# GpSimd waits for the attention tiles of the next batch at their places in its own order

## The reference

```python
pos = clip(base + s_idx * freq_avg + phase_avg, 0, Ll - 1); lo = floor(pos); hi = min(lo + 1, Ll - 1)
g_lo = xh[b_ix, lo]
g_hi = xh[b_ix, hi]
g = g_lo + frac[..., None, None] * (g_hi - g_lo)
out_h = einsum('blshd,blhs->blhd', g, w)
```

## Time and profile before

| | |
|---|---|
| three runs | 2343.15, 2349.13, 2356.42 us (median 2349.13) |
| the profiled execution: span, first to last instruction | 2353.6 us |
| PE busy | 1720.4 us (73%) |
| DVE busy | 1254.1 us (53%) |
| POOL busy | 1103.7 us (47%), nearly all of it 1056 indirect DMAs |
| ACT busy | 988.0 us (42%) |
| mean granted clock of PE | 0.854 |

### The profile page before, as it was taken

How to read it: one execution, slowest core, us unless ns; L and a number is a source line. 1 busy time by engine, 2 the same in 40 slices (tenths; PEclk the granted TensorE clock), 3 DMA queues, 4 the chain that set the end, 5 groups by cost and what they waited for, 6 DMA issues and landing times.

```text
span 2353.6 us, 31786 instructions
## 1 busy us (share of the span) xinstructions
PE 1720.4 (73%) x12145; PEld 1141.7 (49%) x12153; DVE 1254.1 (53%) x2158; ACT 988.0 (42%) x2363; POOL 1103.7 (47%) x1069
## 2 busy tenths in 40 slices
PE   5787876767777766666776766667787768879866
PEld 3354534445445534344555434454455346656645
DVE  6565645555556444555565545655565454343345
ACT  3365673234543551243353540335354533343333
POOL 0000016475556345664556255554665367766630
PEclk8799998778989877988898978789888879989876
DMA  3010023132223232232223232232233343223321
GB/s 133 10 24 14 19 48 96 58 102 83 79 75 103 63 74 79 79 96 73 88 79 90 56 95 70 83 90 72 86 89 85 69 148 99 88 81 90 88 47 36
DMA packets 93420, 178.72 MB, mean 76 GB/s; under 512 B 21452, under 2 KB 50264, under 8 KB 93016
## 3 DMA queue, kind: packets, MB, share of 16 engines
q0 software_dynamic: 50688, 138.48, 21.4%
q1 hardware_dynamic: 42584, 38.23, 5.8%
HBM read 151.46 MB, written 9.44 MB: 68 GB/s over the span
## 4 chain that ended last, share of the span: by engine, by line
PE 39%; DVE 19%; another core or an unknown queue 18%; ACT 12%; issue 9%; SPq 1%; POOL 1%; DMA 1%; DVEq 0%; POOLq 0%; ACTq 0%
PE c L1612 5%; DVE pool_c L1235 4%; PE pa L1508 3%; PE pb L1508 3%; PE ta L1542 2%; DVE ssq L1132 2%; PE ta L1516 2%; ACT pool_a L771 2%; ACT pool_a L836 2%; PE sc L1587 2%; DVE pool_a L1155 1%; DVE pool_a L1185 1%; PE tb L1389 1%; PE pb L1560 1%
## 5 line engine op out<-in xcount | busy, mean ns | idle before, releaser
L729 POOL DMA_INDIRECT pool_c<-rows_of_x,idx x1056 | 1100.9, 1043 | 1156.5 <-PE c L1612 380.0
L1612 PE MATMUL c<-ident,pool_c 128*128 128x128 f32 x2112 | 337.1, 303 | 61.6 <-DVE pool_c L1235 32.2
L1612 PEld LDWEIGHTS c<-ident,pool_c 128*128 128x128 f32 x2112 | 278.3, 158 | 143.0 <-issue 97.0
L1235 DVE TENSOR_TENSOR pool_c<-pool_c 128x768 f32<-128x768 f32 x352 | 331.3, 951 | 20.1 <-DMA pool_c<-rows_of_x,idx 19.7
L860 ACT ACTIVATE prob<-sc,nmax 128x128 f32<-128x128 f32 x512 | 179.3, 374 | 0.1
L1516 PE MATMUL ta<-ident,pool_a 128*128 128x128 f32 x512 | 90.9, 333 | 90.8 <-DVE pool_a L1155 80.4
L771 ACT COPY pool_a<-tb 128x512 f32<-128x512 f32 x188 | 112.5, 599 | 103.6 <-remote 58.3
L1155 DVE TENSOR_TENSOR pool_a<-ta,rinv 128x512 f32<-128x512 f32 x64 | 44.3, 692 | 199.9 <-remote 158.3
L1542 PE MATMUL ta<-vmix,pool_a 128*64 128x64 f32 x1024 | 80.9, 239 | 81.0 <-ACT pool_a L771 67.5
L1142 DVE TENSOR_REDUCE nmax<-sc 128x8 f32<-128x1024 f32 x64 | 77.5, 1211 | 103.9 <-remote 96.1
L1508 PE MATMUL pa<-wqkv,pool_a 128*128 128x512 f32 x192 | 118.8, 706 | 12.9 <-DVE pool_a L1185 7.4
(11 more groups left out here) (413 smaller groups left out, 3344.3 us busy)
## 6 DMA issues: line engine op xcount, KB each, us to landing
pool_c<-rows_of_x,idx POOLq DMA_INDIRECT x1056
vmix<-vring SPq DMA_DIRECT2D x128, 128.0 KB
rows_of_x<-x2tok SPq DMA_DIRECT2D x16, 256.0 KB
xtok<-in_x SPq DMA_DIRECT2D x4, 512.0 KB
x_of_all<-x2tok SPq DMA_DIRECT2D x8, 256.0 KB
out<-pool_c SPq DMA_DIRECT2D x8, 256.0 KB, 2.3
wqkv<-in_wqkv SPq DMA_DIRECT2D x1, 1536.0 KB
xtok<-x_of_all SPq DMA_DIRECT2D x3, 512.0 KB
```

The costliest lines, as they stand in the source:

```text
L729: pool.indirect_dma_start(gat[:, n % GB, s, :], None, tables[b % 2], bass.IndirectOffsetOnAxis(ap=idx[:, t, SC * c + s:SC * c + s + 1], ax ...
L1235: V.tensor_tensor(g4, g4, wv, ALU.mult).then_inc(SEM["c_prod"], 1)
L1612: ins = mm(out[:, c:c + P], x, ident[:], start=(i == 0 and k == 0), stop=(i == BCH - 1 and k == len(parts) - 1), is_transpose=True, skip_g ...
```

## The change

POOL's function `first` now waits at the steps "S" and "O": it holds POOL's list at that place until PE has written the tile's scores, or its probabilities times values. Gathers that come later in the list are issued after the wait. No other engine's code is changed.

```diff
@@ -710,7 +710,8 @@
             pool.wait_ge(setup["pool"], 1)
 
             def first(b, what, *a):
-                pass
+                if what in ("S", "O"):
+                    wait_filled(pool, (what, *a), b)
 
             def gather(b, n):
 
```

## The result

On the chip of the first comparison the kernel after takes 2323.71 us (median of 8 runs, 2319.04 to 2339.86) and the kernel before 2352.03 (8 runs, 2339.13 to 2361.38): a ratio of 0.9895, 95% interval 0.9865 to 0.9925. The ratios in this document come from executions in the chip's faster state alone, and lie up to 0.3% from the quotient of the medians (here 0.988). The change makes the kernel about 1% faster. I had predicted no change, with a chance of 0.05 for faster.

A forecast was written before the change was run, and what follows sets the result against it. The prediction took the kernel as bound by the to and fro between PE, DVE and ACT. Its terms 0 + 0 + 0 left the median of 2349.13 unmoved: forecast 2349 us, range 2338 to 2361.

The forecast's parts named there:

- None of the 90 gathers is held by a tile: Gathers of chunks 31 to 87, batches 0 to 2, behind one new wait: tile already signalled when needed; cost 0.
- A met wait costs 0, by chunk 21's 0.30 us: Chunk 21's gather, already with a second wait, starts after the usual 0.30 us pause, so an extra met wait adds 0.00.
- Chunk 44: Gather with a second, long met wait; its pause of 0.69 to 1.80 us was not put down to that wait.
- my bounds: Cost of one met wait on POOL: taken as 0, upper end 1.50 us, no lower end below nothing.
- What hides it: Each of the 90 gathers leads its product by at least 11.64 us; POOL has some 119 us per batch to catch up.
- Rival 1: Chunks 31 to 87, batches 0 to 2: POOL pays per wait until the lead is gone; 2382 to 2449 us, chance 0.04.
- Rivals 2 and 3: A tile holds gathers, 2889 us, chance 0.01; last batch's seven product waits vanish or double, 2329 or 2369, chance 0.05.
- Nothing waits on POOL but those products: Only the products using the gathers were taken to depend on POOL, and SP's DMA queues not to move.
- a lower end below nothing has no ground, since no work leaves POOL: The new waits on POOL were taken to be unable to make the kernel faster.

The follow-up runs named there:

- met: Kernel before, with POOL waiting at the change's 128 places for a semaphore met since the kernel's start: ratio 0.9874.
- rest3: Kernel before, with an already met wait ahead of the sum's wait at batch 3's 82 gathers from chunk 6 on only: ratio 1.0013.
- rest: Kernel before, with an already met wait ahead of the sum's wait at the 238 gathers from chunk 6 on that the change leaves alone: ratio 1.0117.
- again: The changed kernel run again on another chip, against the kernel before: ratio 0.9887.
- late5: Kernel before, with gathers of chunks 31 to 87 in batches 0 to 2 waiting for the sum of one chunk later, no added instruction: ratio 0.9894.
- late4: Kernel before, with gathers of chunks 31 to 87 in batches 0 to 2 waiting for the sum of two chunks later: ratio 0.9898.
- swap: Kernel before, with an already met wait put behind the sum's wait at the same 90 gathers, so the gather keeps the sum's wait: ratio 0.9989.
- pad_end: Kernel before, with the same 128 waits all issued behind POOL's last gather, none between gathers: ratio 0.9994.
- null: The kernel before, unchanged, timed against itself: 2302.20 us, ratio 0.9969.
- spaced: Kernel before, with POOL clearing the next gather's buffer part and waiting between a chunk's three gathers (chunks 31 to 87, batches 0 to 2): 2207.10 us, ratio 0.9554.
- touch: Kernel before, with POOL clearing only one column and waiting between a chunk's three gathers (chunks 31 to 87, batches 0 to 2): 2320.42 us, ratio 0.9895.
- both: The change's 128 waits together with late5's shift by one chunk, against the kernel before: ratio 0.9962.
- none: Kernel before without the 513 gathers of chunks 31 to 87 in batches 0 to 2 and their products' waits: 2070.77 us, ratio 0.8970.
- third: Kernel before, issuing one of each chunk's three gathers for chunks 31 to 87 of batches 0 to 2: ratio 0.9056.

## Why the prediction was wrong

- *"None of the 90 gathers is held by a tile"*: right. No tile's matmul releases a gather in the waits of after, and met, which can be held by nothing, gives the same time.
- *"A met wait costs 0, by chunk 21's 0.30 us"*: wrong where POOL has run dry. There the sum's wait, now a separate instruction, lets the gather go about 0.75 us behind the sum instead of 0.27. Chunk 21 came in an unbroken run, where nothing shows. Chunk 44 had that very delay within its pauses in the earlier trace rows (0.69 us and more), and I explained it away: by the trace's semaphore updates its gather starts 0.74 us behind the update of its sum in all four batches, where gathers with one wait start 0.26 us behind. The size, 0.4 to 0.5 us at the gathers that POOL idles for, was inside my bounds.
- *"What hides it", the lead of 11.64 us*: right. It falls to 6.49, and no product of batches 0 to 2 waits.
- *Rival 1* (the front of POOL pays until the lead is used up): the price was real, the path wasn't. *Rivals 2 and 3* did not occur: what follows batch 2 changed by 2.4 us in the two profiled executions, and rest3 gives 1.0013.
- **The step that failed**: *"Nothing waits on POOL but those products"*, and with it *"a lower end below nothing has no ground, since no work leaves POOL"*. POOL's gathers act on PE, and through its late signals on DVE, with no semaphore between POOL and PE: without 513 of them the time falls by 10.3%, with a longer pause between them by 4.5%. Once that coupling exists, a shift of the gathers can move the time in either direction. The runs with a shift lie between 0.9874 (met) and 1.0117 (rest). The evidence stood in the profile that I had read: the chain of the earlier trace rows gives 18% to releases that could not be placed and 9% to "issue". I took both as background of the to and fro between the engines. It stood in the earlier trace rows as well: the sum ends at 794.96 us, POOL is idle from 795.79, and the gather starts only at 796.75. The sum's semaphore is updated at 796.50, 1.54 us behind PE's end.
- **What is shown, and what isn't.** Shown: the change gains by the later start of the gathers of chunks 31 to 87 (after, again, met, late5 and late4 within 0.9874 to 0.9898; swap and pad_end none), PE's signals come late beside gathers, and gathers cost the kernel time in a way that depends on how closely they follow each other. Argued only: that the 1% is this coupling at work, the gathers falling better between the attention steps. No trace shows it: PE's signal is over 1 us late for 42 of the 48 tiles in after as in before (37 in null), and the unplaced waits of the two tile steps are 237.1 us in after, between null's 212.3 and before's 254.4. Nor do the gathers follow each other less closely. Of the 513, the number that starts within 0.35 us of the one before is 412 in before, 416 in after and 407 in late5. It drops to 158 in spaced, and to 86 in touch, whose pause is 0.38 us (420 start within 0.45 us there, and 158 in spaced). Open: which tiles gain, why rest loses and both gains so little, and what the gathers and PE share.
- **The clock.** With less idle time goes a higher clock. Mean granted clock: 0.854 in before and 0.856 in null, 0.877 in spaced, 0.893 in none. PE's busy time in none is 1627.5 us for the same matmuls, 92.9 less than in the earlier trace rows and 83.1 less than null's 1710.6. So part of the 234 us is idle time that is gone, and part goes with the clock. The executions ran on different chips, and how much of those 83 to 93 us lies on the path isn't known.

## What to carry to other kernels

An engine off the critical path is not free because nobody waits for its results. Leave a stretch of it out once and see what the others gain. Here "remote" idle time on DVE and "issue" idle time on PE beside unbroken runs of gathers was the sign, and the times of the semaphores' updates named the engine that was late. A pause of 0.60 us in place of 0.30 between gathers gave 4.5%. And an extra wait in front of an instruction can move the critical wait into an instruction of its own: put the wait that is met last first in the code, so that it stays on the instruction.

## What the runs showed of the hardware

- A second or third gather of a chunk, 0.30 us behind the one before, cost the kernel 0.64 us each (third); the first ones, left out as well, 0.12 us each (none). Neither an eighth of the bytes (0.9999) nor an eighth of the rows (1.0112) makes the kernel faster.
- Beside gathers PE's semaphore update for a tile's scores comes 2.45 us behind the end that the profile gives (median of 48 tiles of before, up to 12.46); with no gathers near it comes 0.04 us behind (16 tiles of batch 0). DVE's and ACT's updates come within 0.02 us of their ends throughout.
- The durations of the others' instructions hardly change: DVE is busy 1254.1 us in before, 1247.1 in none; ACT 988.0 and 980.5. What DVE and ACT lose is idle time in front of instructions. The Trainium skill's page "SBUF — State Buffer", section "Who interferes with whom", says that DVE and GpSimd share a pair of ports, that certain DVE instructions and a GpSimd instruction block each other there for a whole instruction, and that on trn2 a tensor_reduce never contends. The maximum (L1142) is a TENSOR_REDUCE and takes 1.211 us on average in before and 1.195 in none; so the trace agrees. Its start is up to 12.4 us late all the same, because PE's signal is; that is outside what the rule names.
- A released gather whose sum's wait is a separate semaphore instruction starts some 0.75 us behind the sum; with the wait on the gather itself, 0.27 us.
